# State space convolution in two blocks of 128 steps, context products ahead of the inverse, experts handed over by bank

## The chip, the cores and the metric

One core of a Trainium2 chip runs the whole program. The metric is device time in microseconds of one execution. Its engines each take their own instructions in program order and wait for one another by semaphores: PE (TensorE, matrix products and transposes), DVE (VectorE), ACT (ScalarE), POOL (GpSimd) and SP, which only issues DMAs. All data is fp32; a matmul call with fp32 operands shows as two MATMUL records in the trace.

## What is computed

x has 16 items of 256 steps and 256 channels. Six residual branches follow one another: windowed attention, attention to a context of 77 rows, a mixture of 8 experts (one for each row), an RWKV layer (time mixing by a scan over the 16 items, then channel mixing), a block with top-32 attention to the context, FiLM and a state space layer, and a product with signs of weights. The change is about the state space layer of the fifth and about the experts of the third:

```
def s4d(x, log_dt, A_re, A_im, C_re, C_im, D_skip):       # x: [16, 256, 256]
    ...
    K = 2.0 * jnp.einsum('dn,dnl->dl', dC, powers).real    # a kernel of 256 steps a channel
    n = 2 * L
    Kf = jnp.fft.rfft(K, n=n, axis=-1)
    xf = jnp.fft.rfft(x, n=n, axis=1)
    y = jnp.fft.irfft(xf * Kf.T[None], n=n, axis=1)[:, :L] # causal convolution
    return y + x * D_skip

h = jax.nn.gelu(jnp.einsum('td,edf->etf', xf, W1) + b1[:, None, :], approximate=False)
y_all = jnp.einsum('etf,efd->etd', h, W2) + b2[:, None, :]  # experts; the top one counts
```

## The kernel before

The program has stages one after another: attention and router (to about 448 us), placing the rows by expert, the experts (518 to 865 us), and the last stage (866 to 1935 us), which does all of the fourth to the sixth branch.

*Experts* (expert_blocks, L829). 39 blocks of 128 rows. For a block PE does first (4 calls to p_u, two banks of 512 columns), turn_rows, second (8 calls) and turn (8 transposes of u to p_uT); DVE adds b1 to both banks in one instruction (add_b1, L1018), ACT applies gelu to both in one (L1222). PE's order is turn(i), first(i+1), turn_rows(i+2), second(i). In the gaps of DVE it also works out the state space kernel K and its spectrum (spectrum_product, L1318).

*Last stage* (mixing_and_state_space, L1359). A software pipeline over the 16 items with 20 iterations n. In iteration n the engines work on five items at once: t=n (time mixing), c=n-1 (channel mixing), j=n-2 (top-32 attention and FiLM), i=n-3 (state space and its network), p=n-4 (norm and sign product). From n=4 to n=15 all five are there. The order of each engine's work is written out by hand in one loop per engine: PE at L2330, DVE at L1836, ACT at L2077, POOL at L1563.

PE's order in an iteration is keys_D, turn_2, scores, values_D, receptance_D, forward, receptance, channel (first half), turn_6, channel (second half), inverse, turn_1(t+1), project, context, channel_out 0, turn_3, channel_out 1, hidden 0, out_product, hidden 1, network, turn_average, film, turn_E, queries_keys. Most products share few PSUM banks: p_Y serves inverse, project, channel_out, out_product and network one after another, and each has to wait until the one before was read.

The convolution goes over the frequency domain. forward multiplies u (256 steps) by cosines and sines at 256 complex frequencies (8 calls into p_U), DVE multiplies p_U by the two halves of the spectrum (spectrum, L1773, to tA and tB), POOL adds and subtracts (L1512, L1513), inverse goes back (8 calls to p_Y). tA lies in the tile of mix. DVE's scale_out (L1781) is the reader of the inverse.

DVE's order in an iteration is add_network, difference, scores, new_maximum, norm_out, add_channel_mix, take 0, spectrum, take 1, numerator (waits for ACT's exponentials, L1979), scale_out, denominator, output, invert, take 2, gated, take 3, finish (L1697), stats_E, residual, average, add_mix, stats_1, film, keys. A take is 8 MAX8 and 8 MATCH_REPLACE instructions. PE's out_product waits for gated and for finish, since its bank p_Y holds channel_out's result until then. PE's turn_1(t+1) waits for ACT's n_1(t+1) (L1912), which stands behind exps_D in ACT's order:

```
            def turn_1(n, t):
                pe.wait_ge(d["n1"], t + 1)
...
            def out_product(n, t):
                pe.wait_ge(d["rw"], t + 1)
                latest(pe, (z["g2"], n - 1), (d["gate"], n))
...
            def scale_out(i):
                dve.wait_ge(e["yp"], i + 1)
```

## Time and profile before

| | us |
|---|---|
| median of 3 runs | 1937.6 (1936.95 to 1940.23) |
| profiled execution | 1936.92 |
| its span | 1935.2 |
| experts, 520 to 860: PE busy | 336.2 of 340 |
| last stage, 1150 to 1320: PE busy | 167.4 of 170 |

A timeline row has the start, the time from the start of the first to the end of the last of the merged instructions, engine, line and operation, what it writes from what, and in brackets how long the engine idled before it and who released it. PE's instructions overlap, so the next group starts some 0.1 to 0.2 us before the end of the one before; what counts is the distance of two starts. PEclk is the granted clock of TensorE as a share of full speed.

### The profile page before, as it was taken

To read this page: it belongs to the slowest core of one execution; us is meant where nothing else is said; L and a number is where in the kernel's file an instruction comes from. 1 tells how busy PE (TensorE), PEld (TensorE's weight loads), DVE (VectorE), ACT (ScalarE), POOL (GpSimd) and SP (SyncE) were. 2 spreads that over 40 slices of the span, in tenths; PEclk is the share of its full clock that TensorE was granted. 3 is DMA by queue.
4 is the path that set the end of the run, shared out by engine and by line. 5 is a ranking of instruction groups with operands and counts; after the bars stand their busy time and mean duration, and the time that the engine had idled before them with its cause. 6 is when DMAs were issued, how large, how long until landed. Compare 5 with 4: busy or idle time off the path is not lost.

```text
span 1935.2 us, 26723 instructions
## 1 busy us (share of the span) xinstructions
PE 1686.4 (87%) x8210; PEld 1308.0 (68%) x8210; DVE 1287.0 (67%) x4141; ACT 864.3 (45%) x1675; POOL 605.3 (31%) x984
## 2 busy tenths in 40 slices
PE   5899999992299999982779999999999999999775
PEld 3677777771166677761658778778778778777654
DVE  3567777762148777334478888889888889876642
ACT  1444444440031111114556766667766667754321
POOL 1111111213300000005534445545444544433211
PEclk9899999995699999995789999999999999999987
DMA  9000000006644343425000000000000000000000
GB/s 272 3 1 1 1 1 1 1 1 234 249 137 137 110 119 99 134 77 197 12 6 1 12 12 6 12 6 12 12 12 6 12 6 7 6 6 1 6 6 11
DMA packets 81573, 94.11 MB, mean 49 GB/s; under 512 B 19142, under 2 KB 69527, under 8 KB 81179
## 3 DMA queue, kind: packets, MB, share of 16 engines
q1 hardware_dynamic: 72747, 78.91, 12.7%
q0 software_dynamic: 3072, 8.39, 1.2%
q10 hardware_dynamic: 5616, 5.11, 0.8%
q8 instruction: 69, 1.13, 0.2%
q14 instruction: 69, 0.57, 0.1%
HBM read 71.94 MB, written 20.45 MB: 48 GB/s over the span
## 4 chain that ended last, share of the span: by engine, by line
PE 35%; DVE 13%; ACT 2%; issue 2%; POOL 2%; POOLq 0%; ACTq 0%
PE E_pY L2313 6%; PE E_pK L2204 5%; PE E_pU L2303 4%; PE E_pK L2163 3%; PE E_pY L2151 3%; PE E_pS L2266 3%; PE E_pY L2284 3%; PE E_pU L2275 2%; DVE E_wk L1738 2%; DVE E_ex L1670 2%; DVE E_m L1731 1%; PE E_pY L2163 1%; PE E_pT L2145 1%; DVE E_num L1677 1%; PE E_pY L2214 1%
## 5 line engine op out<-in xcount | busy, mean ns | idle before, releaser
L1222 ACT ACTIVATE F_uT<-F_puT 128x1024 f32<-128x1024 f32 x39 | 39.9, 1024 | 294.3 <-PE F_puT L1282 294.3
L1492 POOL TENSOR_SCALAR E_var<-E_mv 128x2 f32<-128x2 f32 x80 | 34.2, 427 | 355.9 <-DVE E_mv L1607 355.7
L1273 PE MATMUL F_pu<-C_W,F_hT 128*128 x312 | 143.9, 605 | 0.3 <-issue 0.3
L1291 PE MATMUL F_py<-C_W,F_uT 128*128 x624 | 141.2, 379 | 1.2 <-ACT F_uT L1222 1.2
L1291 PEld LDWEIGHTS F_py<-C_W,F_uT 128*128 128x128 f32 x624 | 115.6, 190 | 16.0 <-issue 1.9
L2214 PE MATMUL E_pY<-E_Wcv,E_hid 128*128 128x256 f32 x512 | 118.7, 386 | 3.3 <-issue 3.3
L2303 PE MATMUL E_pU<-E_xT,E_W 128*128 128x256 f32 x512 | 117.7, 385 | 2.3 <-ACT E_xT L2052 2.3
L2313 PE MATMUL E_pY<-E_W,E_hid 128*128 128x256 f32 x512 | 118.1, 379 | 0.0
L2204 PE MATMUL E_pK<-E_cmix,E_Wck 128*128 128x256 f32 x512 | 115.8, 379 | 1.3 <-ACT E_hid L1993 1.3
L2214 PEld LDWEIGHTS E_pY<-E_Wcv,E_hid 128*128 128x128 f32 x512 | 96.0, 192 | 27.8 <-issue 15.6
L2303 PEld LDWEIGHTS E_pU<-E_xT,E_W 128*128 128x128 f32 x512 | 98.7, 193 | 16.7 <-ACT E_xT L2052 2.9
L2204 PEld LDWEIGHTS E_pK<-E_cmix,E_Wck 128*128 128x128 f32 x512 | 96.1, 190 | 14.5 <-ACT E_hid L1993 2.1
L989 POOL TENSOR_SCALAR F_var<-F_mv 128x1 f32<-128x1 f32 x39 | 8.7, 223 | 302.7 <-DVE F_mv L1001 302.7
L2313 PEld LDWEIGHTS E_pY<-E_W,E_hid 128*128 128x128 f32 x512 | 95.0, 190 | 12.1 <-issue 0.5
L2060 ACT ACTIVATE E_hid<-E_pU,b 128x256 f32<-128x256 f32 x128 | 53.8, 471 | 105.0 <-PE E_pU L2303 105.0
L1273 PEld LDWEIGHTS F_pu<-C_W,F_hT 128*128 128x128 f32 x312 | 57.6, 195 | 58.9 <-issue 58.8
L222 POOL TENSOR_SCALAR A_varB<-A_mvB 128x2 f32<-128x2 f32 x16 | 3.5, 218 | 280.3 <-DVE A_mvB L261 280.3
L1018 DVE TENSOR_TENSOR F_u<-F_pu,F_b 128x1024 f32<-128x1024 f32 x39 | 47.8, 1225 | 54.2 <-PE F_pu L1273 54.1
L1738 DVE MATCH_REPLACE8 E_wk<-E_m,E_wk 128x77 f32<-128x77 f32 x384 | 80.5, 225 | 0.0
L2163 PE MATMUL E_pK<-E_mix,Wkvr 128*128 128x256 f32 x256 | 67.0, 409 | 8.4 <-DVE E_mix L1640 8.4
L1761 DVE TENSOR_TENSOR E_u<-E_u,E_pS 128x256 f32<-128x256 f32 x32 | 13.5, 422 | 85.5 <-PE E_pS L2266 85.5
L581 PE MATMUL A_pqa<-A_hTB,A_Wq 128*128 128x256 f32 x256 | 64.9, 399 | 5.1 <-ACT A_hTB L430 5.1
(402 smaller groups left out, 4353.9 us busy)
## 6 DMA issues: line engine op xcount, KB each, us to landing
F_b<-in_L_ffn_b SPq DMA_DIRECT2D x39, 512.0 KB, 4.4
C_W<-in_L_ffn_W SPq DMA_DIRECT2D x16, 1024.0 KB, 14.0
sorted_x<-zero SPq DMA_DIRECT2D x1, 4992.0 KB, 19.5
F_xs<-sorted_x SPq DMA_DIRECT2D x39, 128.0 KB, 2.4
F_b<-in_L_ffn_b SPq DMA_DIRECT2D x39, 128.0 KB, 3.1
sorted_y<-F_y ACTq DMA_DIRECT2D x39, 128.0 KB, 2.3
out<-E_tB SPq DMA_DIRECT2D x16, 256.0 KB, 2.1
X<-in_x SPq DMA_DIRECT2D x3, 1024.0 KB, 10.7
```

What stands on the lines that cost most here:

```text
L581: last = te.matmul(p_qa[:, half, (m % 2) * S:(m % 2 + 1) * S], Wq[:, kb, m * P:(m + 1) * P], hTB[:, kb, :], start=kb == 0, stop=kb == KD - 1)
L1273: last = nc.tensor.matmul(p_u[:, f, :], hT[:, i % 2, kb, :], W1[:, bass.ds(e, 1), kb, f * 512:(f + 1) * 512], start=kb == 0, stop=kb == KD ...
L1291: last = nc.tensor.matmul(p_y[:, 0:D], uT[:, f, :], W2[:, bass.ds(e, 1), f, :], start=f == 0, stop=f == FB - 1)
L1738: last = v.match_replace(wk[:, t, hd, :], m8[:, turn, t, hd, :], src[:, t, hd, :], TAKEN)
L2151: last = te.matmul(p_Y[:, a, :], x[:, kb, a * P:(a + 1) * P], W[:, kb, :], start=kb == 0, stop=kb == KD - 1)
L2163: last = te.matmul(to[:, o, :], Wkvr[:, m, kb, o * P:(o + 1) * P], mix[:, m, kb, :], start=kb == 0, stop=kb == KD - 1)
L2204: last = te.matmul(p_K[:, q, :], Wck[:, kb, fb * P:(fb + 1) * P], cmix[:, 0, kb, :], start=kb == 0, stop=kb == KD - 1)
L2214: last = te.matmul(p_Y[:, a, :], hid[:, fb, a * P:(a + 1) * P], Wcv[:, fb, :], start=fb == 0, stop=fb == FB - 1)
L2266: last = te.matmul(p_S[:, q, :], amT[:, t * P:(t + 1) * P], w["VW"][:, q * 512:(q + 1) * 512], start=True, stop=True)
L2284: last = te.matmul(p_Y[:, a, :], inv[:, q, a * P:(a + 1) * P], tA[:, q, :], start=q == 0, stop=q == 3)
L2303: last = te.matmul(p_U[:, q, :], W1[:, kb, fb * P:(fb + 1) * P], xT[:, kb, :], start=kb == 0, stop=kb == KD - 1)
L2313: last = te.matmul(p_Y[:, a, :], hid[:, fb, a * P:(a + 1) * P], W2[:, fb, :], start=fb == 0, stop=fb == FB - 1)
```

## The change

The convolution is cut into two blocks of 128 steps. Each block is transformed by itself at 128 complex frequencies (forward and inverse 4 calls each instead of 8). The first block of the result is the product of the first block of u with the first of K; the second takes the second block of u with the first of K, and the first block of u with a spectrum (spec 2 and 3) made of both blocks of K. So DVE has two more products of 512 columns, written to tC and tD (the tiles u and x1), POOL two more sums. tA gets a tile of its own. spectrum stands ahead of take 0 on DVE. On PE, turn_1 and context stand ahead of inverse, both channel_out ahead of turn_3, and out_product ahead of hidden 0. At the start of the last stage, POOL's gathers and first norm go ahead of some memsets. In the experts' stage, add_b1, gelu, first, turn and second go by halves, each with a semaphore of its own. The matrices of the transforms shrink.

```diff
@@ -868,14 +868,14 @@
         g_in, b_in = other[:, 1024:1280], other[:, 1280:1536]
-        fwd = spare[:, 0:1024].rearrange("p (k f) -> p k f", k=KD)
+        fwd = spare[:, 0:256]
...
@@ -950,7 +950,7 @@
                 e = sp.value_load(owner[0:1, i:i + 1], min_val=0, max_val=E - 1)
-                past(sp, s["u"], i - 2)
+                past(sp, s["u1"], i - 2)
                 sp.dma_start(b1[:, i % 2, :], args["L0_ffn_b1"][bass.ds(e, 1)].rearrange("a f -> (a f)").partition_broadcast(P)
...
@@ -1008,15 +1008,16 @@
                 dve.wait_ge(s["hTp"], i + 1)
-                past(dve, s["up"], i - 2)
+                past(dve, s["up1"], i - 2)
                 ve.tensor_copy(hT[:, i % 2], p_hT[:, 0:D].rearrange("p (k q) -> p k q", k=KD)).then_inc(s["hT"], 1)
...
             def add_b1(i):
-                dve.wait_ge(s["up"], i + 1)
                 dve.wait_ge(dma[f"b1{i % 2}"], 16 * (i // 2 + 1))
-                past(dve, s["uTp"], i - 1)
-                ve.tensor_tensor(u[:].rearrange("p (a f) -> p a f", a=2), p_u[:],
-                                 b1[:, i % 2, :].rearrange("p (a f) -> p a f", a=2), ALU.add).then_inc(s["u"], 1)
+                for f in range(2):
+                    dve.wait_ge(s[f"up{f}"], i + 1)
+                    past(dve, s[f"uTp{f}"], i - 1)
+                    cols = slice(512 * f, 512 * f + 512)
+                    ve.tensor_tensor(u[:, cols], p_u[:, f, :], b1[:, i % 2, cols], ALU.add).then_inc(s[f"u{f}"], 1)
...
@@ -1156,7 +1157,9 @@
                 dve.wait_ge(c["spec"], 1)
-                ve.tensor_copy(spec.rearrange("p (h f) d -> p h (f d)", h=2), p_k2).then_inc(c["spec"], 1)
+                step(ve.tensor_copy(spec[:, 0:2].rearrange("p f d -> p (f d)"), p_k2[:, 0, :]))
+                ve.tensor_tensor(spec[:, 2], p_k2[:, 1, 0:D], spec[:, 1], ALU.add)
+                ve.tensor_tensor(spec[:, 3], p_k2[:, 1, D:2 * D], spec[:, 0], ALU.subtract).then_inc(c["spec"], 1)
...
@@ -1217,10 +1220,11 @@
             def gelu(i):
-                act.wait_ge(s["uTp"], i + 1)
                 past(act, s["yp"], i - 1)
-                nc.scalar.activation(uT[:].rearrange("p (a b) q -> p a (b q)", a=2), p_uT[:],
-                                     ACT.Gelu).then_inc(s["uT"], 1)
+                for f in range(2):
+                    act.wait_ge(s[f"uTp{f}"], i + 1)
+                    nc.scalar.activation(uT[:, 4 * f:4 * f + 4, :].rearrange("p b q -> p (b q)"), p_uT[:, f, :],
+                                         ACT.Gelu).then_inc(s[f"uT{f}"], 1)
...
@@ -1267,27 +1271,29 @@
                 pe.wait_ge(s["hT"], i + 1)
-                past(pe, s["u"], i - 1)
-                for kb in range(KD):
-                    for f in range(2):
+                for f in range(2):
+                    past(pe, s[f"u{f}"], i - 1)
+                    for kb in range(KD):
                         last = nc.tensor.matmul(p_u[:, f, :], hT[:, i % 2, kb, :],
...
                                                 start=kb == 0, stop=kb == KD - 1)
-                last.then_inc(s["up"], 1)
+                    last.then_inc(s[f"up{f}"], 1)
             def turn(i):
-                pe.wait_ge(s["u"], i + 1)
-                past(pe, s["uT"], i - 1)
-                for f in range(FB):
-                    last = nc.tensor.transpose(p_uT[:, f // 4, (f % 4) * P:(f % 4 + 1) * P],
-                                               u[:, f * P:(f + 1) * P], k["ident"][:])
-                last.then_inc(s["uTp"], 1)
+                for half in range(2):
+                    pe.wait_ge(s[f"u{half}"], i + 1)
+                    past(pe, s[f"uT{half}"], i - 1)
+                    for f in range(4 * half, 4 * half + 4):
+                        last = nc.tensor.transpose(p_uT[:, half, (f % 4) * P:(f % 4 + 1) * P],
+                                                   u[:, f * P:(f + 1) * P], k["ident"][:])
+                    last.then_inc(s[f"uTp{half}"], 1)
...
                 e = pe.value_load(owner[0:1, i:i + 1], min_val=0, max_val=E - 1)
-                pe.wait_ge(s["uT"], i + 1)
                 past(pe, s["y"], i - 1)
                 for f in range(FB):
+                    if f % 4 == 0:
+                        pe.wait_ge(s[f"uT{f // 4}"], i + 1)
                     last = nc.tensor.matmul(p_y[:, 0:D], uT[:, f, :], W2[:, bass.ds(e, 1), f, :],
...
@@ -1319,10 +1325,10 @@
                 pe.wait_ge(c["late"], 32)
-                for f in range(4):
-                    for kb in range(2):
-                        last = nc.tensor.matmul(p_k2[:, f // 2, (f % 2) * D:(f % 2 + 1) * D], fwd[:, kb, f * P:(f + 1) * P],
-                                                KT[:, kb, :], start=kb == 0, stop=kb == 1)
+                for kb in range(2):
+                    for part in range(2):
+                        last = nc.tensor.matmul(p_k2[:, kb, part * D:(part + 1) * D], fwd[:, part * P:(part + 1) * P],
+                                                KT[:, kb, :], start=True, stop=True)
                 last.then_inc(c["spec"], 1)
...
@@ -1412,7 +1418,7 @@
         fo, tB = sb("fo", [P, 2, D]), sb("tB", [P, 4, D])
-        tA = mix[:, 0:2].rearrange("p m a q -> p (m a) q")
+        tA, tC, tD = sb("tA", [P, 4, D]), u[:], x1[:]
         n3, xb = sb("n3", [P, 2, D]), sb("xb", [P, 2, D])
...
@@ -1509,8 +1515,11 @@
                 pool.wait_ge(e["tAB"], i + 1)
-                g.tensor_tensor(tA[:, 0:2], tA[:, 0:2], tB[:, 2:4], ALU.subtract).then_inc(e["Y"], 1)
-                g.tensor_tensor(tA[:, 2:4], tA[:, 2:4], tB[:, 0:2], ALU.add).then_inc(e["Y"], 1)
+                chained(g.tensor_tensor(tB[:, 2:4], tB[:, 2:4], tD, ALU.add))
+                chained(g.tensor_tensor(tA[:, 2:4], tA[:, 2:4], tC, ALU.add))
+                settled()
+                g.tensor_tensor(tA[:, 0:4:2], tA[:, 0:4:2], tB[:, 1:4:2], ALU.subtract).then_inc(e["Y"], 1)
+                g.tensor_tensor(tA[:, 1:4:2], tA[:, 1:4:2], tB[:, 0:4:2], ALU.add).then_inc(e["Y"], 1)
...
@@ -1545,9 +1554,13 @@
             gather(0)
-            for x in (aa[:], bb[:], mixB[:, 1], cmixB[:, 1]):
+            for x in (aa[:], bb[:], mixB[:, 1]):
                 g.memset(x, 0.0).then_inc(d["init"], 1)
             g.memset(pp[:], -1e38).then_inc(d["init"], 1)
+            gather(1)
+            first(0)
+            gather(2)
+            g.memset(cmixB[:, 1], 0.0).then_inc(d["init"], 1)
             pool.wait_ge(d["init"], 5)
...
@@ -1556,9 +1569,6 @@
                 pool.wait_ge(d["init"], 7 + hd)
-            gather(1)
-            first(0)
-            gather(2)
             first(1)
...
@@ -1768,11 +1778,13 @@
                     dve.wait_ge(f["out"], 16 * (i - 1))
-                for part, dst in ((0, tA), (1, tB[:])):
-                    kf = fourier["spec"][:, 2 * part:2 * part + 2, :].rearrange("p b d -> p (b d)")
-                    last = v.tensor_tensor(dst.rearrange("p (a b) d -> p a (b d)", a=2),
-                                           p_U[:].rearrange("p (a b) d -> p a (b d)", a=2),
-                                           kf.unsqueeze(1).to_broadcast([P, 2, 2 * D]), ALU.mult)
+                past(dve, d["xx1"], min(i + 2, B - 1))
+                past(dve, d["n2"], min(i + 2, B - 1))
+                for part, dst in ((0, tA[:]), (1, tB[:])):
+                    v.tensor_tensor(dst, p_U[:], fourier["spec"][:, part:part + 1, :].to_broadcast([P, 4, D]), ALU.mult)
+                for part, dst in ((2, tC), (3, tD)):
+                    last = v.tensor_tensor(dst, p_U[:, 0:2], fourier["spec"][:, part:part + 1, :].to_broadcast([P, 2, D]),
+                                           ALU.mult)
                 last.then_inc(e["tAB"], 1)
...
@@ -1830,11 +1842,13 @@
             columns()
             stats_1(0)
             masks()
-            dve.wait_ge(d["init"], 10)
             stats_1(1)
+            dve.wait_ge(d["init"], 4)
             add_mix(0)
             for n in range(B + 4):
                 t, c, j, i, p = n, n - 1, n - 2, n - 3, n - 4
+                if n == 1:
+                    dve.wait_ge(d["init"], 10)
                 if n == 3:
                     sign_and_scale()
                     dve.wait_ge(lw["third"], 80)
...
@@ -1850,11 +1864,10 @@
                     norm_out(p)
                 if 0 <= c < B:
                     add_channel_mix(c)
-                if 0 <= j < B:
-                    take(j, 0)
                 if 0 <= i < B:
                     spectrum(i)
                 if 0 <= j < B:
+                    take(j, 0)
                     take(j, 1)
                 if t < B:
                     numerator(t)
...
@@ -2007,7 +2020,8 @@
                 act.wait_ge(e["rsE2"], j + 1)
-                past(act, e["Up"], j - 1)
+                if j >= 1:
+                    act.wait_ge(e["Y"], 2 * j)
                 again(hE[:, j % 2], u, rsE, e["n1"])
...
@@ -2033,6 +2047,8 @@
                 act.wait_ge(e["amp"], j + 1)
+                if j == 0:
+                    act.wait_ge(d["init"], 10)
                 a_.activation(amT[0:J, :], p_T[0:J, 0, :], ACT.Copy).then_inc(e["amT"], 1)
...
@@ -2270,19 +2285,19 @@
                 past(pe, e["g11"], i - 1)
-                for q in range(4):
-                    for a in range(2):
-                        last = te.matmul(p_U[:, q, :], fourier["fwd"][:, a, q * P:(q + 1) * P], u[:, a, :],
-                                         start=a == 0, stop=a == 1)
+                for a in range(2):
+                    for part in range(2):
+                        last = te.matmul(p_U[:, 2 * a + part, :], fourier["fwd"][:, part * P:(part + 1) * P], u[:, a, :],
+                                         start=True, stop=True)
                 last.then_inc(e["Up"], 1)
...
                 for a in range(2):
-                    for q in range(4):
-                        last = te.matmul(p_Y[:, a, :], inv[:, q, a * P:(a + 1) * P], tA[:, q, :],
-                                         start=q == 0, stop=q == 3)
+                    for part in range(2):
+                        last = te.matmul(p_Y[:, a, :], inv[:, part, :], tA[:, 2 * a + part, :],
+                                         start=part == 0, stop=part == 1)
                 last.then_inc(e["yp"], 1)
...
@@ -2353,27 +2368,25 @@
                     turn_6(n, p)
                 if 0 <= c < B:
                     channel(n, c, 1)
+                if t + 1 < B:
+                    turn_1(n, t + 1)
+                if 0 <= j < B:
+                    context(j)
                 if 0 <= i < B:
                     inverse(n, i)
-                if t + 1 < B:
-                    turn_1(n, t + 1)
                 if 0 <= p < B:
                     project(n, p)
-                if 0 <= j < B:
-                    context(j)
                 if 0 <= c < B:
                     channel_out(n, c, 0)
+                    channel_out(n, c, 1)
                 if 0 <= i < B:
                     turn_3(n, i)
-                if 0 <= c < B:
-                    channel_out(n, c, 1)
-                if 0 <= i < B:
-                    hidden(i, 0)
                 if n == 0:
                     pe.wait_ge(lw["first"], 16 * 8)
                 if t < B:
                     out_product(n, t)
                 if 0 <= i < B:
+                    hidden(i, 0)
                     hidden(i, 1)
                     network(n, i, 0, 0, FB)
                 if 0 <= j < B:
...
@@ -2452,9 +2465,9 @@
-    angle = _np.outer(_np.arange(S), (_np.pi / 2 + 2 * _np.pi * _np.arange(S)) / S)
+    angle = _np.outer(_np.arange(P), (_np.pi / 2 + 2 * _np.pi * _np.arange(P)) / P)
     forward = _np.concatenate([_np.cos(angle), _np.sin(angle)], axis=1)
-    for name, a in (("fourier", forward), ("fourier_inverse", forward.T / S)):
+    for name, a in (("fourier", forward), ("fourier_inverse", forward.T / P)):
         arrays["in_" + name] = _np.ascontiguousarray(a.astype(_np.float32))
...
     out = nc.dram_tensor("out_0", (B, S, D), F32, kind="ExternalOutput").ap()

```

## Rows read from the trace of the kernel before

**Rows 1.** The page: busy time, share of the span and instructions of each engine.

```profile
PE 1686.4 (87%) x8210; PEld 1308.0 (68%) x8210; DVE 1287.0 (67%) x4141; ACT 864.3 (45%) x1675; POOL 605.3 (31%) x984
```

**Rows 2.** Windows: length, then busy (count) of PE, PEld, DVE, ACT, POOL; PEclk.

```profile
1150.00:1320.00 170.00, 167.42 (x757) 134.38 (x756) 142.92 (x477) 113.10 (x234) 84.71 (x131) 1.00 0.03 10
```

**Rows 3.** Timeline of PE, one iteration: start, us, line, out<-in, [idle before <-releaser].

```profile
1304.69 1.99 PE L2163 MATMUL E_pK<-E_mix,Wkvr 128*128 128x256 f32 x8
...
1311.45 3.62 PE L2275 MATMUL E_pU<-E_u,E_fwd 128*128 128x256 f32 x16
...
1320.53 3.62 PE L2204 MATMUL E_pK<-E_cmix,E_Wck 128*128 128x256 f32 x16
...
1323.98 3.62 PE L2284 MATMUL E_pY<-E_mix,E_inv 128*128 128x256 f32 x16
...
1327.43 0.60 PE L2145 MATMUL E_pT<-ident,E_n1D 128*128 128x128 f32 x4
...
1328.47 1.96 PE L2151 MATMUL E_pY<-E_sign,E_xT 128*128 128x256 f32 x8 [0.44 <-DVE E_fo L1781]
...
1330.27 1.88 PE L2244 MATMUL E_pS<-E_Wvf,cxT 128*77 128x512 f32 x4
...
1333.10 3.72 PE L2214 MATMUL E_pY<-E_Wcv,E_hid 128*128 128x256 f32 x16
...
1344.81 1.97 PE L2151 MATMUL E_pY<-E_Wo,E_num 128*128 128x256 f32 x8 [0.30 <-DVE E_gate L1697]
...
1362.58 1.99 PE L2163 MATMUL E_pK<-E_mix,Wkvr 128*128 128x256 f32 x8
...
1709.94 1.99 PE L2163 MATMUL E_pK<-E_mix,Wkvr 128*128 128x256 f32 x8
```

**Rows 4.** Timeline of DVE in the same iteration.

```profile
1313.47 1.22 DVE L1731 MAX8 E_m<-E_sc 128x8 f32<-128x77 f32 x8
...
1316.46 1.22 DVE L1773 TENSOR_TENSOR E_mix<-E_pU,E_spec 128x1024 f32<-128x1024 f32 x1
...
1324.63 0.69 DVE L1657 TENSOR_TENSOR E_diff<-E_ex,E_val 128x512 f32<-128x512 f32 x1 [2.90 <-ACT E_ex L1979]
...
1327.63 0.69 DVE L1781 TENSOR_TENSOR E_fo<-E_pY,E_fo 128x512 f32<-128x512 f32 x1 [0.38 <-PE E_pY L2284]
...
1343.99 0.68 DVE L1697 SCALAR_TENSOR_TENSOR E_gate<-E_gate,E_pY 128x512 f32<-128x512 f32 x1
```

**Rows 5.** Timeline of ACT in the same iteration.

```profile
1316.84 0.60 ACT L1989 ACTIVATE E_gate<-E_pY 128x512 f32<-128x512 f32 x1 [0.38 <-PE E_pY L2151]
...
1320.29 0.60 ACT L1993 ACTIVATE E_hid<-E_pK 128x512 f32<-128x512 f32 x1 [0.41 <-PE E_pK L2204]
...
1324.50 0.89 ACT L1912 ACTIVATE E_n1D<-E_hD,E_rs2D 128x256 f32<-128x256 f32 x2
```

**Rows 6.** Timeline of POOL in the same iteration: a sum of the spectrum.

```profile
1318.89 1.27 POOL L1512 TENSOR_TENSOR E_mix<-E_mix,E_tB 128x512 f32<-128x512 f32 x1 [3.87 <-DVE E_tB L1773]
```

**Rows 7.** Windows (columns as in rows 2) within and behind idle times of PE.

```profile
999.00:1003.00 4.00, 0.00 (x0) 0.00 (x0) 3.79 (x10) 1.09 (x2) 3.39 (x10) 1.00 0.01 2
...
1003.00:1005.00 2.00, 0.17 (x1) 0.17 (x2) 1.97 (x3) 0.00 (x0) 1.92 (x3) 0.50 0.00 0
...
1773.80:1776.30 2.50, 0.00 (x0) 0.00 (x0) 2.43 (x7) 0.00 (x0) 1.07 (x1) 1.00 0.00 0
```

**Rows 8.** Timeline of PE: restarts after two idle times.

```profile
941.24 8.83 PE L2214 MATMUL E_pY<-E_Wcv,E_hid 128*128 128x256 f32 x32 [2.04 <-issue]
...
1836.75 6.63 PE L2284 MATMUL E_pY<-E_mix,E_inv 128*128 128x256 f32 x16 [4.34 <-POOL E_mix L1513]
```

**Rows 9.** Timelines at the end of the experts and the last stage's start.

```profile
861.33 3.72 PE L1291 MATMUL F_py<-C_W,F_uT 128*128 x16 [1.20 <-ACT F_uT L1222]
...
878.68 0.25 DVE L1607 BATCH_NORM_AGGREGATE E_mv<-E_st 128x2 f32<-128x6 f32 x2
...
880.53 0.23 POOL L1492 TENSOR_SCALAR E_var<-E_mv 128x2 f32<-128x2 f32 x1
```

More of the change, by code:

```diff
@@ L1374, in mixing_and_state_space @@
              "VW": sb("VW", [J + 1, 4 * D])}
-        fourier = {"fwd": sb("fwd", [P, 2, 2 * S]), "spec": sb("spec", [P, 4, D])}
-        inv, Wq, Wk = sb("inv", [P, 4, S]), sb("Wq", [P, KD, P]), sb("Wk", [P, 2, P])
+        fourier = {"fwd": sb("fwd", [P, 2 * P]), "spec": sb("spec", [P, 4, D])}
+        inv, Wq, Wk = sb("inv", [P, 2, P]), sb("Wq", [P, KD, P]), sb("Wk", [P, 2, P])
         W1, W2 = sb("W1", [P, KD, DM]), sb("W2", [P, FB, D])
```

7 lines of the change are left out of this document (3 added, 4 removed).

## Prediction

> **What bounds the kernel now.** I read the page's busy times first [rows 1]: PE is busy for 87% of the span, DVE 67%. A stretch of the second half [rows 2] shows the stage that the change is about: PE 98% busy at clock 1.00, DVE 84%, POOL 50%. Then the order of PE's work in one iteration [rows 3]. With 0 at the first of keys_D (1304.69), the next iteration's keys_D starts at 57.89, and the sixth after that at 1709.94, again 57.89 apart; the same spacing holds back to iteration 4. PE idles for less than 1 us in it (2.6 of the 170 us of [rows 2]), 0.44 before project (for DVE's L1781) and 0.30 before out_product (for DVE's L1697) among it. So PE bounds the stage by a hair: the second row of that pair says that DVE's chain ends just as PE arrives. That chain [rows 4] is the second thing to see: from L1781 (22.94 on my scale) to the end of L1697 (1343.99 + 0.68, so 39.98) DVE works without a gap, 17.04 us, and out_product starts 0.14 later, at 40.12. DVE takes its work in program order, so all of that (statistics, denominator, output, the reciprocal, two takes, gated, finish) is queued behind scale_out, which waits for the inverse.
>
> **The change part by part.** *Matmuls.* forward and inverse go from 8 matmul calls to 4 each. Before, each took 3.45 us of PE's queue (1323.98 to 1327.43 [rows 3]), so each gives back 1.73: 3.45 us an item, 55 us over 16 items if PE alone set the time. The products of the spectrum in the experts' stage halve too, once: 1.7.
>
> *DVE's products.* Two of 1024 columns at 1.22 become two of 1024 and two of 512; the nearest 512-column row out of PSUM is 0.69 (L1781) [rows 4]. Back to back that is 3.5 us instead of 2.3, +1.3 an item. They move ahead of take 0, which starts at 8.78. The forward now ends at 6.76 + 1.73 = 8.5, so they need no wait and end at 12.3. Takes 0 and 1 follow, 3.0 each (1313.47 to 1316.46), and end at 18.3, before the exponentials that numerator waits for (19.94 before, L1657, 19.1 now by the next step but one). No cost on the path.
>
> *POOL's sums.* Two at 1.27 become four in sequence [rows 6], 5.1 us: the spectrum is ready at 12.3 + 5.1 + 0.1 = 17.5. A slower POOL pass (say 1.7 each) gives 19.3. The Trainium skill (GPSIMD Engine Reference, Key points) says that POOL shares its SBUF interfaces with VectorE and contends with DVE instructions that have two SBUF inputs. The rows show 1.27 beside takes, so no sign of it here; if it held, the later value is the one to use, and the inverse below starts at 23.2 either way.
>
> *PE's order up to the inverse.* Nothing before forward changes, so all engines are where they were at 6.76. channel's second half then ends at 19.29 - 1.73 = 17.56. Next stands turn_1, which used to follow the inverse at 22.74. It waits for n_1(t+1) on ACT, whose end before was 1324.50 + 0.89, 20.70 [rows 5]. ACT is busy nearly all the way from the falls to there; only the 0.38 and 0.41 that it waited for PE disappear. So n1D is ready at 19.9 and turn_1 waits 2.3 us, with context and the inverse queued behind it. turn_1 0.44, context 2.83 (1330.27 to 1333.10), inverse 1.73: the inverse starts at 23.2 and ends at 24.95, against 22.74 before. Although it is 1.73 shorter and needs nothing before 17.5, it ends 2.2 us later.
>
> *DVE's chain.* scale_out starts 0.20 after that, at 25.15 instead of 22.94. DVE has finished numerator at about 21.8 and stands idle for 3.3 us with the whole chain queued behind it. Then the unchanged 17.04: L1697 ends at 42.2, out_product starts at 42.35.
>
> *PE after the inverse.* Before, turn_1, project, context, channel_out, turn_3 and hidden's first half lay beside DVE's chain, 16 us. Now it is project (1.80, from 0.84 after L1781 starts), channel_out twice 3.45 and turn_3 0.44. PE is through with these at 35.1 if project starts at once, at up to 36.3 with its wait for L1781 and channel_out's for DVE to read project's bank, and waits at out_product for 6 to 7 us. context stands ahead of the chain and hidden's first half behind it. hidden's 3.45 is not covered any more: from out_product on, the old 1344.81 to 1362.58 (17.77) plus 3.45. The next keys_D starts at 42.35 + 17.77 + 3.45 = 63.6. **+5.7 us an iteration.** Put as one cycle: +2.2 (inverse later) and +3.45 (hidden behind out_product).
>
> *The clock.* In the stage before no idle time of PE reaches a microsecond; now one of 6 to 7 comes in each iteration. PE idled from 999.0 on: for 4 us the granted clock was 1.00 (2.4 GHz), then 0.50 (1.2 GHz) [rows 7]. Restarted at 0.50, the inverse at 1836.75 took 6.63 for 16 instructions that take 3.62 at full clock (3.0 lost), and 32 of channel_out at 941.24 took 8.83 instead of 7.07, twice 3.62 less the overlap (1.8 lost) [rows 8]. I take 2.4, between the two, in each iteration; it falls on out_product and hidden, which nothing hides. Its bounds are 0 and 3. An idle time of 2.5 (1773.8) left the clock at 1.00 [rows 7], while one of 2.0 stands before 941.24, which then ran slow [rows 8]: for turn_1's wait of 2.3 I add 0.4, a quarter of 1.8. Together **+8.5 an iteration, 66.4**.
>
> *Experts.* The stage runs without idle time on PE in the steady state, so handing over by bank has nothing to give there: at its end PE waited 1.20 for the whole gelu [rows 9], of which some 0.9 go, and a little at the start and at the few blocks with long DVE work. With the 1.7 of the spectrum I take -4, between -2 and -7. DVE's two adds of 512 cost 0.1 more a block, beside PE's work. The value of SP's biases waits only for the later of the two banks, as before.
>
> *Start of the last stage.* POOL's gather(1), and with it first(0), moves ahead of seven memsets (cmixB's to the last of heads'); first(0) started at 880.53 though its input was ready at 878.93 (878.68 + 0.25) [rows 9]: -1.6, which goes through to turn_1 and keys. The memsets moved behind it are awaited only in iterations 1 and 2. The transforms' matrices shrink by 768 KB, which can only help the gathers. -1.6, between 0 and -4.
>
> *Tail.* In iterations 16 to 18 there is no out_product. Less inverse and context ahead of it (where PE waited 4.34 for POOL's sums [rows 8]) gain; POOL's 2.5 and DVE's 1.3 lose in the last, where nothing is beside them. I estimate -3, between -8 and +3.
>
> **The sum.** The profiled execution took 1936.9 (span 1935.2 and 1.7 around it), 0.7 below the median of the three. Twelve iterations (4 to 15) at +8.5 are 102; iteration 3 has no project and no output on DVE and starts its chain earlier, for it I take +6. 1936.9 + 102 + 6 - 4 - 1.6 - 3 = 2036; against the median 2037. **Predicted: 2036 us**, 5% slower.
>
> **Rivals.** *A, PE's work is what counts (faster, 0.10).* The Trainium skill (Perfetto Trace Analysis, Identifying the Most-Contended Engine) says to improve the engine with the highest occupancy first, and that is PE. As a mechanism of this kernel: if DVE's chain were done before PE reaches out_product, all 3.45 would come back in 13 iterations: 1936.9 - 45 - 9 = 1883. For it speaks 98% in [rows 2]; against it that the chain of 17.04 would have to fit beside 9.2 us of PE work. It decides from the point where the inverse ends below 17 or 18 on my scale. *B, the waits but a steady clock (slower, 0.22).* +5.7: 12 x 5.7 + 4 = 72, minus 8.6: 2001. For it speaks the idle time of 2.5 at full clock; against it that 4 us of idling sufficed for the fall. *C, the waits largely vanish (0.08).* ACT's exponentials could come early enough that turn_1 waits for little, and the chain starts near 22; then only hidden's 3.45 less what PE gained is left, and the time is between 1930 and 1975. *D, the clock falls twice in each iteration (slower, part of the forecast's own spread).* Another 1.4 an iteration: 2053. My forecast, with the clock falling at out_product, has 0.60.
>
> **Range and chances.** 1985 to 2056: it takes in B with its bounds (2001 less 8 and more), the forecast and D, and leaves out A and most of C. Whether a change can be told from none is a matter of about 0.2%, some 4 us. Faster 0.12 (A and an edge of C), same 0.02, slower 0.86.
>
> **What would show it.** Right: keys_D 63 to 67 us apart in iterations 4 to 15; idle time of PE before L1697's user, out_product, of some 6 us in each, put down to DVE's finish; about 2 us before turn_1, put down to ACT's n1D; DVE idle some 3 us before scale_out, put down to the inverse; a half clock at the start of out_product. PE's busy time falls in instructions by 64 + 64 pairs, but the share falls well below 98%. Wrong: a spacing near 54, or the inverse starting before 20, or PE waiting for POOL's sums instead of n1D. The experts' stage should keep its length within a few us.

## The result and the profile after

The kernel after takes 2025.5 us (median of 4 runs, 2022.8 to 2027.4) where the kernel before takes 1937.3 (4 runs, 1934.9 to 1940.2): a ratio of 1.0454, with a 95% interval of 1.0434 to 1.0474. The forecast was 2036, in a range of 1985 to 2056.

The page of after, span and busy times, answers to [rows 1]. The third is its group of instructions for out_product (busy, mean ns of one, idle time before them and its releaser); before, the same group had 33.2 us busy, 405 ns for one, and 14.2 us of idle time, 6.6 of it put to DVE's finish.

```profile
span 2025.1 us, 26432 instructions
PE 1667.5 (82%) x7946; PEld 1275.5 (63%) x7946; DVE 1302.7 (64%) x4214; ACT 865.2 (43%) x1714; POOL 644.1 (32%) x1016
L2166 PE MATMUL E_pY<-E_Wo,E_num 128*128 128x256 f32 x128 | 53.1, 588 | 86.6 <-DVE E_gate L1707 79.0
```

PE issues 264 matmul records fewer and is busy 18.9 us less, though some of them now run on the slow clock, and the span is 89.9 us longer. The loss is idle time: 79.0 us in front of out_product alone. The same stretch as [rows 2]:

```profile
1150.00:1320.00 170.00, 142.46 (x615) 111.20 (x614) 130.85 (x464) 105.26 (x213) 83.86 (x119) 0.95 0.03 9
```

PE goes from 167.4 to 142.5 busy in 170 us, DVE from 142.9 to 130.9, and the granted clock from 1.00 to 0.95: no engine is busy nearly all the time any more. What sets the time is a ring of waits: each engine waits for a step of another that itself waits, and the circle closes once an iteration.

One iteration of PE after (start, duration, line, tiles, calls, in brackets the idle time and its releaser), the answer to [rows 3]. I count from its keys_D, 1338.04:

```profile
1338.04 1.99 PE L2178 MATMUL E_pK<-E_mix,Wkvr 128*128 128x256 f32 x8
1344.80 1.89 PE L2290 MATMUL E_pU<-E_u,E_fwd 128*128 128x256 f32 x8
1352.78 3.72 PE L2219 MATMUL E_pK<-E_cmix,E_Wck 128*128 128x256 f32 x16
1357.77 0.66 PE L2160 MATMUL E_pT<-ident,E_n1D 128*128 128x128 f32 x4 [1.26 <-ACT E_n1D L1925]
1358.26 1.88 PE L2259 MATMUL E_pS<-E_Wvf,cxT 128*77 128x512 f32 x4
1361.09 1.99 PE L2299 MATMUL E_pY<-E_tA,E_inv 128*128 128x256 f32 x8
1363.96 1.97 PE L2166 MATMUL E_pY<-E_sign,E_xT 128*128 128x256 f32 x8 [0.88 <-DVE E_fo L1793]
1366.93 7.14 PE L2229 MATMUL E_pY<-E_Wcv,E_hid 128*128 128x256 f32 x32 [1.01 <-DVE E_tB L1826]
1373.91 0.60 PE L2160 MATMUL E_pT<-ident,E_n 128*128 128x128 f32 x4
1380.29 3.39 PE L2166 MATMUL E_pY<-E_Wo,E_num 128*128 128x256 f32 x8 [5.78 <-DVE E_gate L1707]
1383.52 7.07 PE L2318 MATMUL E_pU<-E_xT,E_W 128*128 128x256 f32 x32
1402.94 1.35 PE L2178 MATMUL E_pK<-E_mix,Wkvr 128*128 128x256 f32 x5
```

The next keys_D is 64.90 later, where it was 57.89. forward and inverse are half as long (1.89 for 3.62). But turn_1 waits for ACT at 19.73, the inverse starts at 23.05 behind it, and out_product at 42.25 after 5.78 us of nothing, with both halves of hidden still to come. out_product itself takes 3.39 for 1.97.

VectorE and GpSimd in the same iteration, the answers to [rows 4] and [rows 6]:

```profile
1346.82 1.22 DVE L1784 TENSOR_TENSOR E_tA<-E_pU,E_spec 128x1024 f32<-128x1024 f32 x1
1349.68 0.68 DVE L1786 TENSOR_TENSOR E_x<-E_pU,E_spec 128x512 f32<-128x512 f32 x1
1363.12 0.69 DVE L1793 TENSOR_TENSOR E_fo<-E_pY,E_fo 128x512 f32<-128x512 f32 x1 [3.55 <-PE E_pY L2299]
1379.47 0.68 DVE L1707 SCALAR_TENSOR_TENSOR E_gate<-E_gate,E_pY 128x512 f32<-128x512 f32 x1
```
```profile
1350.44 1.28 POOL L1518 TENSOR_TENSOR E_tB<-E_tB,E_x 128x512 f32<-128x512 f32 x1 [2.08 <-DVE E_x L1786]
1353.04 1.27 POOL L1521 TENSOR_TENSOR E_tA<-E_tA,E_tB 128x512 f32<-128x512 f32 x1
```

DVE idles 3.55 until the inverse is done; from scale_out (25.08) to the end of finish, which is L1707 now and was L1697 (42.11), it runs 17.03 without a gap, as before (17.04). POOL's fourth sum starts at 1354.27 and ends 17.50 after keys_D, 5.5 before the inverse uses it.

### The profile page after: what moved, and what is told of

It reads as the page before. It is cut to its first block, busy times and chain, and to the rows that moved or that the text cites. A ratio compares the mean times of both kernels' runs of the same rounds, so it can differ in the third digit from the quotient of the medians.

```text
span 2025.1 us, 26432 instructions
## 1 busy us (share of the span) xinstructions
PE 1667.5 (82%) x7946; PEld 1275.5 (63%) x7946; DVE 1302.7 (64%) x4214; ACT 865.2 (43%) x1714; POOL 644.1 (32%) x1016
## 4 chain that ended last, share of the span: by engine, by line
PE 31%; DVE 14%; ACT 7%; issue 4%; POOL 1%; DMA 0%; ACTq 0%; POOLq 0%; DVEq 0%
PE E_pU L2318 6%; PE E_pY L2328 5%; PE E_pY L2166 3%; PE E_pK L2178 3%; PE E_pS L2281 3%; DVE E_wk L1748 2%; DVE E_ex L1680 2%; PE E_pY L2299 2%; DVE E_m L1741 2%; PE E_pT L2160 1%; PE E_pY L2178 1%; PE E_pK L2219 1%; PE E_pS L2259 1%; DVE E_num L1687 1%; ACT E_cmixB L1931 1%
## 5 line engine op out<-in xcount | busy, mean ns | idle before, releaser
L1498 POOL TENSOR_SCALAR E_var<-E_mv 128x2 f32<-128x2 f32 x80 | 40.9, 512 | 433.9 <-DVE E_mv L1617 433.6
L1226 ACT ACTIVATE F_uT<-F_puT 128x512 f32<-128x512 f32 x78 | 42.8, 595 | 287.4 <-PE F_puT L1287 249.4
L2166 PE MATMUL E_pY<-E_Wo,E_num 128*128 128x256 f32 x128 | 53.1, 588 | 86.6 <-DVE E_gate L1707 79.0
L2318 PEld LDWEIGHTS E_pU<-E_xT,E_W 128*128 128x128 f32 x512 | 102.5, 201 | 19.9 <-ACT E_xT L2068 4.4
L2166 PEld LDWEIGHTS E_pY<-E_Wo,E_num 128*128 128x128 f32 x128 | 37.6, 308 | 98.3 <-issue 90.4
L1020 DVE TENSOR_TENSOR F_u<-F_pu,F_b 128x512 f32<-128x512 f32 x78 | 52.1, 689 | 41.8 <-PE F_pu L1277 41.6
```

Of the source, the lines that this page charges most:

```text
L1020: ve.tensor_tensor(u[:, cols], p_u[:, f, :], b1[:, i % 2, cols], ALU.add).then_inc(s[f"u{f}"], 1)
L2166: last = te.matmul(p_Y[:, a, :], x[:, kb, a * P:(a + 1) * P], W[:, kb, :], start=kb == 0, stop=kb == KD - 1)
L2318: last = te.matmul(p_U[:, q, :], W1[:, kb, fb * P:(fb + 1) * P], xT[:, kb, :], start=kb == 0, stop=kb == KD - 1)
```

## The experiments

The theory is that of the prediction. In the last stage a ring runs through PE's order up to the inverse, through scale_out and DVE's chain to out_product, and back to the next keys_D. The place of hidden decides whether its work fills PE's wait or stands behind it, and the clock adds a term. Rivals: the longer products and sums cost the time, PE's own work sets it, or hidden's place is free.

**1. The order of before on the new transforms.** The two lines list the order of PE's steps; they are not the code.

```diff
-turn_1, context, inverse, project, channel_out 0, channel_out 1, turn_3, out_product, hidden 0, hidden 1
+inverse, turn_1, project, context, channel_out 0, turn_3, channel_out 1, hidden 0, out_product, hidden 1
```

> The kernel after with TensorE's order of before (inverse, turn_1, project, context, channel_out 0, turn_3, channel_out 1, hidden 0, out_product, hidden 1); transforms, products, sums and the experts' stage stay those of after. Theory (the order makes the loss): the inverse starts at 17.6 on the scale with 0 at keys_D and ends at 19.3; scale_out then waits for numerator alone and starts at 21.8, the chain of 17.04 ends at 38.9, out_product starts at 39.0 and 17.8 follow: 56.8 an iteration where after has 64.9. 12 iterations at -8.1 and 6 for iteration 3: 2025 - 103 = 1922, some 15 below before. Rival (the longer work of DVE and POOL on the half-size transforms eats what TensorE gains): 57.9 an iteration or more, 1935 to 1945.

Measured: 1913.2 us (1912.6 to 1916.3), 0.988 of before (0.9863 to 0.9896). Iterations are 56.38 apart in its trace. So the transforms, with all they put on DVE and POOL and with the small gains ahead of the stage, are worth 23 us, and the order alone loses 112. Its PE rows, counted from keys_D at 1354.00:

```profile
1372.29 1.89 PE L2299 MATMUL E_pY<-E_tA,E_inv 128*128 128x256 f32 x8
1376.27 1.97 PE L2166 MATMUL E_pY<-E_sign,E_xT 128*128 128x256 f32 x8 [1.65 <-DVE E_fo L1793]
1385.21 0.66 PE L2160 MATMUL E_pT<-ident,E_n 128*128 128x128 f32 x4 [0.59 <-ACT E_n L1919]
1392.62 1.96 PE L2166 MATMUL E_pY<-E_Wo,E_num 128*128 128x256 f32 x8
```

scale_out follows numerator on DVE without a wait:

```profile
1375.44 0.68 DVE L1793 TENSOR_TENSOR E_fo<-E_pY,E_fo 128x512 f32<-128x512 f32 x1
```

The inverse is at 18.3, not 17.6, without harm: scale_out is held by numerator and starts at 21.44, and out_product finds its input at 38.6. Three waits are left (1.65, 0.59, and 0.26 ahead of receptance). The halved transforms took 3.45 of PE's work and gave 1.5 an iteration, which is how much earlier scale_out starts (22.94 before).

**2. Only out_product back between hidden's halves.**

```diff
+                if 0 <= i < B:
+                    hidden(i, 0)
                 if t < B:
                     out_product(n, t)
                 if 0 <= i < B:
-                    hidden(i, 0)
                     hidden(i, 1)
```

> The kernel after with one edit: out_product goes back between hidden's halves. Theory: out_product starts at 42.3 as in after, but 3.45 of its 5.8 us of waiting are filled by hidden 0, what is left (2.3) is too short for the clock to fall: 64.9 - 3.45 - 1.6 = 59.8 an iteration, 2025 - 61 - 4 = 1960. Rival 1 (the clock falls all the same): 61.4, 1980. Rival 2 (hidden's place does not count, only the late inverse does): 64.9, 2025.

Measured: 1960.9 (1958.4 to 1964.5), ratio 1.0123 (1.0106 to 1.0139); 60.02 apart. out_product stays where it was, 42.24 after keys_D, and takes 1.97:

```profile
1411.61 3.72 PE L2318 MATMUL E_pU<-E_xT,E_W 128*128 128x256 f32 x16 [1.11 <-ACT E_xT L2068]
1416.27 1.97 PE L2166 MATMUL E_pY<-E_Wo,E_num 128*128 128x256 f32 x8 [0.94 <-DVE E_gate L1707]
1434.04 2.00 PE L2178 MATMUL E_pK<-E_mix,Wkvr 128*128 128x256 f32 x8
```

The theory gave 1960, the rivals 1980 and 2025. hidden's place is worth 65 us, its 3.45 and the clock. scale_out starts 25.08 after the keys_D at 1374.03, as in after:

```profile
1399.11 0.69 DVE L1793 TENSOR_TENSOR E_fo<-E_pY,E_fo 128x512 f32<-128x512 f32 x1 [3.55 <-PE E_pY L2299]
```

Taken together, the traces of before and of experiments 1 and 2 show what sets the iteration. scale_out starts at 22.94, 21.44 and 25.08, and the next keys_D comes 34.94 to 34.95 after it in all three, although PE has 3.45 more work an iteration in before than in the other two.

**3. Only the inverse ahead of turn_1 and context.**

```diff
+                if 0 <= i < B:
+                    inverse(n, i)
                 if t + 1 < B:
                     turn_1(n, t + 1)
                 if 0 <= j < B:
                     context(j)
-                if 0 <= i < B:
-                    inverse(n, i)
```

> The kernel after with one edit: the inverse goes ahead of turn_1 and context. Theory: it starts at 17.6 and ends at 19.3; the chain is then held by numerator and starts at 21.8 instead of 25.1; out_product starts at 39.0 instead of 42.3 with 6 us or more of waiting ahead of it, so the clock still falls: 61.6 to 61.8 an iteration, 2025 - 38 - 3 = 1984. Rival (DVE's chain is held by something else that comes at 24 or 25, such as POOL's sums or ACT's gate, and not by the inverse's place): 64.9, 2025.

Measured: 2010.7 (2007.0 to 2013.3), ratio 1.0379 (1.0361 to 1.0396). The sign is right, the size is not: 15 us gained where 41 were expected. Two terms were missing. The first is in DVE's chain, counted from keys_D at 1333.55:

```profile
1354.99 0.68 DVE L1793 TENSOR_TENSOR E_fo<-E_pY,E_fo 128x512 f32<-128x512 f32 x1
1358.86 0.69 DVE L1826 TENSOR_TENSOR E_tB<-E_pY,E_L_ffn_bias 128x512 f32<-128x512 f32 x1 [0.81 <-PE E_pY L2166]
1359.58 1.41 DVE L1828 TENSOR_SCALAR E_tB<-E_tB 128x512 f32<-128x512 f32 x1
1361.03 1.64 DVE L1830 TENSOR_TENSOR E_tB<-E_tB,E_X 128x512 f32<-128x512 f32 x1
1373.06 0.68 DVE L1707 SCALAR_TENSOR_TENSOR E_gate<-E_gate,E_pY 128x512 f32<-128x512 f32 x1
```

scale_out did start at 21.44. But output's first step then waits 0.81 for project, which stands behind context, and its next two take 1.41 and 1.64 where after has 0.43 and 0.69. The chain is 18.75 long instead of 17.03, and out_product starts at 40.3, not 39.0. While DVE waited, POOL had begun the sums of the time mixing's state; its rows beside those two:

```profile
1359.45 1.27 POOL L1527 TENSOR_TENSOR E_bb<-E_ex,E_bb 128x512 f32<-128x512 f32 x1
1360.67 1.45 POOL L1529 TENSOR_TENSOR E_aa<-E_ex,E_aa 128x512 f32<-128x512 f32 x1
1362.09 1.71 POOL L1531 TENSOR_TENSOR E_bb<-E_bb,E_ex 128x512 f32<-128x512 f32 x1
```

Both engines slow down where an elementwise DVE instruction and a POOL sum have all their operands in SBUF, though the first of the three sums keeps its 1.27. It is so in 11 iterations of this run (L1828 1.40 to 1.50); in the twelfth, where no sum stands beside them, L1828 takes 0.43 and L1830 0.69. The reciprocal beside such sums keeps its 3.34. So does an instruction that reads PSUM: in experiment 5 finish (L1707) lies wholly beside a POOL sum of 1.71 (1366.98 to 1368.69) and takes its usual time:

```profile
1367.48 0.68 DVE L1707 SCALAR_TENSOR_TENSOR E_gate<-E_gate,E_pY 128x512 f32<-128x512 f32 x1
```

The other side of it: the chain of after has such a step later (L1687, 1.64 beside POOL's 1.72), which here is 0.69. The trace of before has that one as well (L1677, 1.64 beside POOL's L1531, 1.72 from 1338.88 on); the prediction looked only beside takes and saw no sign of it. The Trainium skill (GPSIMD Engine Reference, Key points) says that POOL shares its SBUF interfaces with VectorE; these rows agree. No run moved POOL's sums alone, so this is read from rows and not tested. The second term is the clock, measured below. Together: out_product 1.3 later than expected and 0.9 more for the clock, times 12, are 26 us.

**4. Keeping TensorE busy in its wait.** 12 matmuls whose result is overwritten, added to after.

```diff
+                if 0 <= i < B and t < B:
+                    pe.wait_ge(e["tAB"], i + 1)
+                    for r in range(12):
+                        te.matmul(p_U[:, r % 4, :], W1[:, 0, 0:P], W1[:, 1, 0:D], start=True, stop=True)
                 if t < B:
                     out_product(n, t)
```

> The kernel after with 12 extra matmuls of 256 columns (5.2 us, their result is overwritten) between turn_3 and out_product in iterations 3 to 15, where TensorE waits 5.8 us. They put no work on any other engine. Theory (the clock is a term of its own): out_product starts at 42.3 as before, now at clock 1.00, takes 1.97 instead of 3.39, and hidden's start is not slow either: 63.3 an iteration, 2025 - 20 = 2005. Rival 1 (the slow start is the first read after a wait, not the clock; or it is hidden by something): 64.9, 2025. Rival 2 (the extra work pushes out_product): above 2025.

Measured: 2006.5 (2003.9 to 2009.0), ratio 1.0361 (1.0344 to 1.0378); 63.47 apart.

```profile
1371.86 1.97 PE L2166 MATMUL E_pY<-E_Wo,E_num 128*128 128x256 f32 x8 [0.59 <-DVE E_gate L1707]
1393.08 1.99 PE L2178 MATMUL E_pK<-E_mix,Wkvr 128*128 128x256 f32 x8
```

More work for PE made the kernel 19 us faster, as the clock term asks. 63.47 is the ring without the clock (the prediction's 63.6), and what after has above it, 1.4, is the clock's. In after it fell at the very end of the wait; granted clock is the third column from the right (window, PE, PEld, DVE, ACT, POOL busy, clock, DMA share, GB/s):

```profile
1379.00:1380.00 1.00, 0.00 (x0) 0.00 (x0) 1.00 (x6) 0.00 (x0) 0.00 (x0) 0.89 0.00 0
1380.00:1381.00 1.00, 0.71 (x2) 0.65 (x3) 0.93 (x3) 0.00 (x0) 0.00 (x0) 0.50 0.00 0
1382.00:1383.00 1.00, 1.00 (x4) 0.72 (x4) 0.00 (x0) 0.00 (x0) 0.80 (x3) 0.50 0.00 0
1383.00:1384.00 1.00, 1.00 (x6) 0.90 (x5) 0.28 (x1) 0.00 (x0) 0.84 (x4) 0.91 0.00 0
```

It went to 0.50 (1.2 GHz) at about 1379.8, half a microsecond before PE restarted, and was back 2.9 after that. In experiment 3 the wait is 6.60, and there it had been down for more than 3 us at the restart (1373.88) and stayed down for 5.7 after it:

```profile
1370.00:1371.00 1.00, 0.00 (x0) 0.00 (x0) 1.00 (x8) 0.43 (x1) 0.00 (x0) 0.50 0.00 0
1378.00:1379.00 1.00, 1.00 (x4) 0.82 (x3) 0.97 (x3) 0.00 (x0) 0.71 (x1) 0.50 0.00 0
1379.00:1380.00 1.00, 1.00 (x5) 0.77 (x5) 0.96 (x4) 0.00 (x0) 0.48 (x1) 0.72 0.00 0
```

**5. The chain shortened by take 3.**

```diff
-                if 0 <= j < B:
-                    take(j, 3)
                 if 0 <= c < B:
                     finish(c)
                     stats_E(c)
                 if t < B:
                     residual(t)
                 if 0 <= j < B:
+                    take(j, 3)
                     average(j)
```

> The kernel after with one edit on VectorE: take 3 (2.9 us) moves from before finish to behind residual, ahead of average, which is its only user. TensorE's order is that of after. Theory (the chain's length sets out_product): out_product starts at 39.4 instead of 42.3, TensorE waits 2.9 instead of 5.8 for it and the clock no longer falls: 39.4 + 21.2 = 60.6 an iteration, 2025 - 52 - 4 = 1970. If the clock falls all the same: 62.2, 1990. Rival (finish waits for channel_out or for another engine and not for the takes): 64.9, 2025. Average comes 2.9 later against residual, but 7 us of hidden cover it.

Measured: 1991.5 (1989.3 to 1993.8), ratio 1.0281 (1.0266 to 1.0297): the branch in which the clock falls all the same. out_product moved from 42.25 to 39.33 and the wait from 5.78 to 2.87, so the chain's length sets it. But the clock did not follow the length of the wait. Two consecutive iterations with the same wait:

```profile
1306.17 3.55 PE L2165 MATMUL E_pY<-E_Wo,E_num 128*128 128x256 f32 x8 [2.86 <-DVE E_gate L1707]
1368.31 1.97 PE L2165 MATMUL E_pY<-E_Wo,E_num 128*128 128x256 f32 x8 [2.87 <-DVE E_gate L1707]
```

In iterations 4 to 15 out_product took 1.97 twice and 2.5 to 3.75 ten times, and the distances between keys_D repeat with a cycle of five: 62.24, 62.13, 60.56, 62.23, 63.53.

**6. The same, kept busy.** 5 such matmuls (2.2 us) in front of out_product.

> The kernel after with take 3 behind residual (as in a_take3_late) and with 5 extra matmuls of 256 columns (2.2 us, their result is overwritten) between turn_3 and out_product, where TensorE waited 2.87. In a_take3_late iterations took 60.56 or, after the very same wait, 62.1 to 63.6. Theory (those differ by the clock alone, which falls in the wait in some iterations and not in others): every iteration 60.56, 1992 - 12 x 1.8 = 1970. Rival (something else lengthens those iterations, or the extra work does): they still vary, 1985 to 1995.

Measured: 1971.7 (1969.2 to 1974.6), ratio 1.0188 (1.0171 to 1.0205). All distances from iteration 4 on are 60.54 to 60.56. The clock is the whole of what varied, and costs 20 us there: from 0 to 3.1 an iteration after one and the same wait of 2.87.

**7. The other side: before, with hidden 0 behind out_product.**

```diff
-                if 0 <= i < B:
-                    hidden(i, 0)
...
                 if t < B:
                     out_product(n, t)
                 if 0 <= i < B:
+                    hidden(i, 0)
                     hidden(i, 1)
```

> The kernel before with one edit: hidden 0 goes behind out_product. Transforms, products, context's place and all else stay. Theory: the chain on VectorE still ends at 40.1, so TensorE waits 3.75 instead of 0.30 for it, and 3.45 more stand behind it: 61.3 an iteration with the clock steady, 1937 + 13 x 3.45 = 1982; with a fall of the clock some 1.6 more in each, 2002. Rival (hidden's place is free, because TensorE's own work sets the time): 57.9, 1937.

Measured: 2007.8 (2007.5 to 2010.4), ratio 1.0373 (1.0357 to 1.0389).

```profile
1370.96 3.54 PE L2151 MATMUL E_pY<-E_Wo,E_num 128*128 128x256 f32 x8 [3.74 <-DVE E_gate L1697]
```

This one move, on the full-size transforms, costs 72 us. One of its iterations (keys_D at 1141.30 and 1202.64) kept the clock and took 61.34, to the hundredth the 57.89 + 3.45; the others took 62.8 to 64.4. A PE that was 98% busy [rows 2] lost 3.7% by an exchange of two of its own steps.

**8. The experts' handover alone, on before.** first, add_b1, turn, gelu and second by halves of 512, as in the change.

```diff
-                dve.wait_ge(s["up"], i + 1)
...
+                for f in range(2):
+                    dve.wait_ge(s[f"up{f}"], i + 1)
+                    past(dve, s[f"uTp{f}"], i - 1)
+                    cols = slice(512 * f, 512 * f + 512)
+                    ve.tensor_tensor(u[:, cols], p_u[:, f, :], b1[:, i % 2, cols], ALU.add).then_inc(s[f"u{f}"], 1)
```

> The kernel before with the experts' handover by bank alone (first, add_b1, turn, gelu and second in halves of 512). Theory as predicted: 0.9 at the end of the stage and a little elsewhere, -2.3: 1934.5. As the traces of before and after read: -0.7 to -0.8, not to be told from no change: 1936. Rival (the second instruction on VectorE and ScalarE and the finer waits cost more than they give): 1938 or more.

Measured: 1937.3 (11 runs) against 1936.0 (21 runs), ratio 1.0007 (0.9998 to 1.0016): no difference that can be told. The last block's wait for the gelu did shrink, from 1.20 [rows 9] to 0.59:

```profile
858.89 3.72 PE L1295 MATMUL F_py<-C_W,F_uT 128*128 x16 [0.59 <-ACT F_uT L1224]
```

**9 and 10. A version that beats both.** First attempt: inverse, context, turn_1, project, both channel_outs, turn_3, hidden 0, out_product, hidden 1; all of take 3 behind residual.

> The kernel after with TensorE's order inverse, context, turn_1, project, channel_out 0 and 1, turn_3, hidden 0, out_product, hidden 1, with take 3 on VectorE behind residual, and with turn_average and film 0 one quarter of a network product later. Theory: the old order on the new transforms (56.4 an iteration) still waits 1.65 ahead of project and 0.59 ahead of turn_3; here context fills the first, the second is gone, some 0.9 of waiting ahead of channel_out comes instead and out_product finds its input: 55.3 an iteration, 1900. Rival (average, now 2.9 later against residual, makes turn_average, film or the next keys_D wait by 2 us or more): 57 or more, 1920 and over.

Measured: 1931.9 (1925.2 to 1933.7), ratio 0.9970 (0.9959 to 0.9982): the rival. out_product found its input at 38.35, with no wait, but PE had come late to it: the two waits of 0.87 and 1.11 below are new, and 0.28 and 0.53 behind out_product are the price of the later average.

```profile
1339.81 3.72 PE L2317 MATMUL E_pU<-E_xT,E_W 128*128 128x256 f32 x16 [1.11 <-ACT E_xT L2067]
1354.17 0.44 PE L2269 MATMUL E_pT<-ident,E_am 128*77 128x128 f32 x2 [0.28 <-DVE E_am L1765]
1359.03 1.96 PE L2280 MATMUL E_pS<-E_VW,E_amT 78*128 78x512 f32 x4 [0.53 <-ACT E_fo L2057]
1388.44 7.14 PE L2228 MATMUL E_pY<-E_Wcv,E_hid 128*128 128x256 f32 x32 [0.87 <-DVE E_tB L1826]
```

The second attempt answers them except for the 0.53, which stays: context is cut in two around project, turn_3 stands before the last quarter of channel_out 1, and only the second half of take 3 moves. Again the two lines are the order, not the code.

```diff
-turn_1, context, inverse, project, channel_out 0, channel_out 1, turn_3, out_product, hidden 0, hidden 1
+inverse, turn_1, context (first half), project, context (second half), channel_out 0, channel_out 1 (3/4), turn_3, channel_out 1 (1/4), hidden 0, out_product, hidden 1
```

> The kernel after with TensorE's order inverse, turn_1, context (its first half), project, context (its second half), channel_out 0, three quarters of channel_out 1, turn_3, the last quarter, hidden 0, out_product, hidden 1, with turn_average and film 0 a quarter of a network product later, and with the second half of take 3 on VectorE (1.45 us) behind residual. Theory: against a_old_order (56.4 an iteration) the wait of 1.65 ahead of project goes, the chain on VectorE is 1.45 shorter, and out_product starts at 37.1 instead of 38.6: 55.0 an iteration, 1897. In the version with all of take 3 behind residual the 0.87 ahead of channel_out, the 1.11 ahead of hidden 0 and 1.2 behind out_product made 57.3. Rival (average, 1.45 later, or ACT's n_3 hold it up as there): 56 or more, 1910 and over.

Measured: 1902.5 (1899.8 to 1911.2), ratio 0.9837 (0.9809 to 0.9866), the fastest of all; 55.43 apart, with out_product at 36.8 and 1.0 us of waiting left in an iteration:

```profile
1381.75 3.72 PE L2329 MATMUL E_pU<-E_xT,E_W 128*128 128x256 f32 x16 [0.25 <-ACT E_xT L2076]
1385.50 1.96 PE L2174 MATMUL E_pY<-E_Wo,E_num 128*128 128x256 f32 x8
```

## Why the prediction was right, and where its sizes were off

The forecast's case came about, with its mechanism. The experiments split the 88 us, to within 1 us: all but the order gives 23 (before to experiment 1), context and turn_1 ahead of the inverse with the later turn_3 cost 48 (experiments 1 to 2), hidden behind out_product costs 65 with its clock (2 to after), of which 19 are the clock (4).

| step, in us | predicted | after |
|---|---|---|
| DVE's four products end | 12.3 | 12.3 |
| POOL's sums ready | 17.5 | 17.50 |
| channel's second half ends (18.29 where the next step follows at once, experiment 1) | 17.56 | 18.46 |
| n1D on ACT, turn_1 starts | 19.9 | 19.73 |
| inverse starts | 23.2 | 23.05 |
| scale_out starts; DVE idle ahead of it | 25.15; 3.3 | 25.08; 3.55 |
| wait ahead of out_product | 6 to 7 | 5.78 |
| out_product starts | 42.35 | 42.25 |
| iteration without the clock | 63.6 | 63.47 (experiment 4) |
| the clock | 2.8 | 1.4 |
| iteration | 66.4 | 64.9 |

- *PE before the inverse.* The one step off by more than 0.3: PE was free 0.7 later (18.29 for 17.56), since receptance now reaches DVE's add of the channel mix (a wait of 0.26) and channel starts later behind it. turn_1's wait, 1.26 instead of 2.3, took it up: what is late next was ACT in either case.
- *The clock, the mis-sized term.* I took 2.4 for out_product and 0.4 for turn_1's wait. turn_1's wait never brought it down, and at out_product it cost 1.4 (2.1 in iteration 4). The reasoning was wrong in kind too. I read "2.5 idle left it at 1.00" and "4 us sufficed" [rows 7] as if the length of the wait decided. Experiments 5 and 6 show that one wait of 2.87 costs anything from 0 to 3.1. The rows allow a mean over iterations, not a price for a wait. After settled by itself into a phase in which the fall came 0.5 us before the restart. The Trainium skill (TensorE: Matmul & The Clock Gate, Part 1: The HAM clock gate) says that the observation behind the clock runs freely, and does not start with the kernel; the cycles of distances in experiments 5 and 7 agree with that.
- *The sum.* In the spans of the two profiled executions: iterations 4 to 14, 78.0 (93.5 predicted); iteration 15, 5.9 up to the next forward (8.5); iteration 3, 6.3 (6); 0.4 in the first three; up to the first keys_D -2.5 (-5.6); the tail 1.9 (-3). Together 89.9 for 99.4. The closeness is in part luck: iterations 4 to 15 were put 18.1 too high, nearly all of it the clock, and the rest together 8.7 too low, so that about half of the error cancelled.
- *Experts and spectrum, -4 predicted.* The spectrum product did give 1.7 (1.89 for 3.62). The handover gave nothing that can be told (experiment 8), where I had 2.3: the 0.6 at the last block stands in the trace, and no row stood behind "a little at the start" and at a few blocks. In the profiled execution of after, 1.6 went back when the clock fell at 639.1, beside the smallest products of the stage (L1319), with PE busy all the time:

```profile
639.00:642.00 3.00, 3.00 (x20) 2.86 (x19) 0.60 (x2) 0.76 (x2) 0.79 (x2) 0.51 0.44 149
```

Chance is a poor account of it. All nine kernels with the new transforms (after, experiments 1 to 6, 9 and 10) have such a fall between 636 and 641 in their traces, and from the start of L1319 to the second turn behind it they take 13.4 or 15.0. The three with the old transforms (before, experiments 7 and 8) have none there and take 11.75. So it very likely belongs to the change; it costs 1.6 to 3.3. The handover does not bring it alone (experiment 8); which other part does stays open.
- *Start of the last stage, -1.6 predicted.* turn_1's idle time ahead of the stage is 17.85 in after and 19.70 in before: 1.8. In the other kernels with the change it is 18.05 to 18.38 and in experiments 7 and 8 19.67 and 19.69, so 1.3 to 1.8.
- *Tail, -3 predicted.* From the forward of iteration 16 to the end, after is 1.9 longer than before; with the old order (experiment 1) it is 3.0 shorter. The cheaper transforms are worth what was predicted, and the order takes it back there too, which I had left out: I priced the tail by the transforms only.
- *A slip.* Four sums of POOL at 1.7 would end at 19.2, not 19.3; nothing hangs on it.

Of the rivals, A (PE's work decides, 1883) fell most clearly. The Trainium skill (Perfetto Trace Analysis, Identifying the Most-Contended Engine) would have the highest occupancy improved first; here its work fell by 3.45 an iteration and the time rose by 88 us, and even in the old order less than half came back (1.5 of 3.45). B (waits, steady clock, 2001) is what experiment 4 made of it: 2006.5. C (waits vanish) and D (two falls) did not come: turn_1 waits 1.26, and no fall of the clock stands beside it.

## What to carry to other kernels

At an engine that is 98% busy the place of each step counts as much as its length: look which step of its list starts another engine's long chain, issue that first, and keep enough of its own independent work between this start and the chain's end. A saving of work on it comes back only as far as it lets the long chain start earlier (here 1.5 of 3.45). When a short step is moved, price what is then issued in front of the chain's start (here 1.26 of waiting and 3.3 of work) and what has moved behind its end (3.45), each as a term of its own.

Where a wait can't be avoided, cover it; a wait of 3 us may cost 3 more through the clock, and another time none.
